# A gated cross-attention block with a quantised feed-forward part: fused mask and row maximum, deviations spread through DRAM, later transposes, another order of the last batches and of the barrier

## The chip, the cores and the metric

The kernel runs on one core of a Trainium2 chip. The metric is device time in microseconds (us), the median of repeated executions. PE is TensorE, DVE is VectorE, ACT is ScalarE, POOL is GpSimd, and SP is the engine that issues most of the transfers.

## The reference

Eight batches (B = 8) of 256 rows (S) of width 256 (D); the context has the same shape; the hidden width I is 704.

```python
# attention: q from layernorm(x), k and v from the context
qh, kh, vh = q @ Wq.T, k @ Wk.T, v @ Wv.T
scores = where(tril, qh @ kh.T / sqrt(256), -inf)
probs = softmax(scores, axis=1)          # over the queries
x = x + tanh(g_xattn) * (probs @ vh)
# feed-forward: every tensor is quantised to 8 bits and scaled back
xq = fake_quant(layernorm(x))            # ONE scale: the maximum over the whole tensor
gate, up = xq @ q(w_gate).T, xq @ q(w_up).T
h = fake_quant(silu(gate) * up)          # again one scale for all of it
x = x + tanh(g_ffn) * (h @ q(w_down).T)
```

The two scales over a whole tensor are barriers: nothing of the hidden layer can be quantised before the last batch's attention is through.

## The kernel before

The host hands over x by rows and x and the context transposed (`xc`), 8 batches each, and all weights. All of it is loaded once, by one list of transfers on SP's queue (lines 286 to 303) and five on ScalarE's (636 to 640), with no wait between them.

The weights Wq and Wk are multiplied into one matrix first (`a_sb`, line 492). Per batch b, on TensorE (loop at line 502):

- `scores(b)`, line 423: context times scaled queries `uT` into PSUM bank SC, transposed so that the softmax runs along the free dimension. It has two column ranges, 256 for the first 128 keys and 128 for the others. Behind each a small bf16 product of the identity and `causal` (line 429) adds -1e30 where the mask is.
- `values(b+2)`, line 396, and `project_queries(b+1)`, line 403, into bank U. The query rows still lack their layernorm factor.
- `spread_deviation(b+2)`, line 412: the factor 1/deviation (`rstd1`, one number per partition) is spread along a row by a product with the identity. ScalarE copies it to `r_bc` (line 644), and VectorE multiplies bank U by it into `uT` (`scale_queries_whole`, line 820).
- `attend(b)`, line 432, which waits for the exponentials and the scaled values, and `transposes2(b-1)`, line 443, the transposes of the second layernorm's result.

VectorE's loop (line 898) does, in this order: residual, statistics and variance of batch b-1 (lines 836 to 854), the two row maxima (826), statistics of batch b+3 (798), a weight maximum (865, or 912 for the down weights), the reciprocal of the softmax sum (832), weight scales, the variance of batch b+3 with its epsilon (806), the scaling of the queries (820), and the largest value of an earlier normalised batch (860). ScalarE's loop (698): exponentials, scaled values, `r_bc`, a copy of the transposes, and quantising one slot of the weights. GpSimd (345): the power -1/2 for both layernorms and the normalising of batches 0 to 5 (`apply2`, 338).

PSUM has eight banks: U, three for values, SC, AT (attention), X2 (transposes) and RB (spread deviations, later turned weights). The gate and up weights are turned by TensorE at batches 6 and 7, the down weights at batch 7, into banks that are free by then.

The last two batches' normalised rows are made by VectorE (line 857, used at 914 and 974). Then come the transposes of batch 7 in two halves (544), the spread of the maximum (`spread_max`, 473) with matmuls on ones around it that keep TensorE running (`keep_warm`, 385), act_scale and act_inv (979), and the quantising of the input (992 to 1019, ScalarE's share 744 to 751). The hidden layer, the second barrier and the down projection follow.

Of the kernel before, what the change touches and what calls it, by code (L numbers as in the profile page):

```python
# [50 lines left out]
def gated_block(nc, x, xc_in, wq_in, wk_in, wvT_in, scalars_in, wgu_in, wd_in, out):  # L51
    assert S == 256 and D == 256 and REST == P // 2 and B == 8 and HALF == 2 * CH

    with ExitStack() as stack:
# [26 lines left out]
        causal = sb("causal", [P, P], BF16)  # L81
# [11 lines left out]
        var1 = sb("var1", [P, B, QT])  # L93
        var2 = sb("var2", [P, B, QT])
        rstd1 = sb("rstd1", [P, B, QT])
        rstd2 = sb("rstd2", [P, B, QT])
        r_bc = [sb(f"r_bc{p}", [P, S]) for p in range(2)]
# [3 lines left out]
        inv_sum = sb("inv_sum", [P, B, QT])  # L101
        probs0 = [sb(f"probs0_{p}", [P, S]) for p in range(2)]
# [3 lines left out]
        xn2T = sb("xn2T", [P, KT, B * S])  # L106
        xmax = sb("xmax", [P, B + 1])
# [14 lines left out]
        wd_diag = sb("wd_diag", [P, KT, P])  # L122
# [21 lines left out]
        U, V0, V1, V2, SC, AT, X2, RB = range(8)  # L144
# [14 lines left out]
        def query_bank(b, f):  # L159

            return bank(V2)[:, 0:S] if b == 0 and f == 1 else bank2(U)[:, f, :]

# [37 lines left out]
        var1_done = sem("var1_done")  # L200
        rstd1_done = sem("rstd1_done")
# [17 lines left out]
        xn2_last = sem("xn2_last")  # L219
# [15 lines left out]
        wguT_last = sem("wguT_last")  # L235
        wd_tr = sem("wd_tr")
        wdT_ready = sem("wdT_ready")
        wd_diag_done = sem("wd_diag_done")
# [36 lines left out]
        def _(sp):  # L275
# [9 lines left out]

            sp.dma_start(ctxT(0), xc_in[0, :, 0]).then_inc(c_here[0], 16)
# [28 lines left out]
        def _(pool):  # L315
# [8 lines left out]
            nc.gpsimd.affine_select(out=causal[:], in_=causal[:], compare_op=ALU.is_ge, fill=MASKED, base=0,  # L324
# [13 lines left out]
            def apply2(b):  # L338
                pool.wait_ge(rstd2_done, b + 1)
# [7 lines left out]
            for b in range(B):  # L347
                if 1 <= b:
                    inverse_deviation2(b - 1)
                if 1 <= b < LAST:  # L350
                    apply2(b - 1)
                if b + 3 < B:
                    inverse_deviation1(b + 3)
            for t in range(QT):
                pool.wait_ge(var2_done, B + t)
                nc.gpsimd.tensor_tensor(rstd2[:, LAST, t:t + 1], var2[:, LAST, t:t + 1], minus_half[:, 0:1],
                                        ALU.pow).then_inc(rstd2_done, 1)

            pool.wait_ge(act_scale_done, 1)
            nc.gpsimd.tensor_scalar(gu_scale[:], wscale[:], act_scale[:, 0:1], None, ALU.mult).then_inc(  # L360
                gu_scale_done, 1)
# [9 lines left out]
            for half in range(2):  # L371
                nc.gpsimd.tensor_scalar(out_scale[:, half, :], wd_row[:], act_scale[:, 1:2], None,
                                        ALU.mult).then_inc(out_scale_done, 1)
# [10 lines left out]
        def _(pe):  # L384
# [27 lines left out]
            def spread_deviation(b):  # L412
# [4 lines left out]
                for t in range(QT):  # L417
                    last = nc.tensor.matmul(bank(RB)[:, t * P:(t + 1) * P],  # L418
# [4 lines left out]
            def scores(b):  # L423
                pe.wait_ge(uT_ready, KT * (b + 1))
                for k, (c0, n) in enumerate(((0, S), (S, P))):
                    for f in range(KT):
                        nc.tensor.matmul(bank(SC)[:, c0:c0 + n], ctxT(b)[:, f, k * P:(k + 1) * P],  # L427
                                         uT[b % 2][:, f, k * P:S], start=(f == 0), stop=False)
                    last = nc.tensor.matmul(bank(SC)[:, c0:c0 + P], ident_bf[:], causal[:], start=False, stop=True)
# [13 lines left out]
            def transposes2(b):  # L443
# [3 lines left out]
                for e in range(KT):  # L447
                    for t in range(QT):
                        last = nc.tensor.transpose(bank2(X2)[:, e, t * P:(t + 1) * P],  # L449
# [14 lines left out]
            def turn_down(n, bk):  # L464
                pe.wait_ge(wd_q_done, 1)
                view = ps[:, bk, :].bitcast(BF16)[:, 0:3 * D].rearrange("p (s h) -> p s h", s=3)
                for s in range(3):
                    i0 = (3 * n + s) * P
                    for t in range(KT):
                        last = nc.tensor.transpose(view[:, s, t * P:(t + 1) * P], wd_q[:, t, i0:i0 + P], ident_bf[:])  # L470
# [31 lines left out]
            for b in range(LAST):  # L502
                scores(b)
                if b + 2 < B:
                    values(b + 2)
                project_queries(b + 1)
                if b + 2 == LAST:
                    pe.wait_ge(wd_diag_done, 1)
                    pe.wait_ge(rbc_ready, LAST)
                    nc.tensor.matmul(bank(RB)[:, S:S + D], ones[:], wd_diag[:].rearrange("p t i -> p (t i)"),  # L510
                                     start=True, stop=True)
                if b + 2 < B:
                    spread_deviation(b + 2)
                if b + 1 == LAST:

                    turn_gate_up(0, VB[(b + 2) % 3])
                    pe.wait_ge(rbc_ready, B)
                    pe.wait_ge(wd_row_ready, 1)
                    turn_gate_up(1, RB)
                attend(b)  # L520
                if b >= 1:
                    transposes2(b - 1)

            p = LAST % 2
            last_value_bank = VB[LAST % 3]
            spare = VB[(LAST - 1) % 3]
            scores(LAST)
            turn_gate_up(2, U)
            turn_down(0, spare)
            pe.wait_ge(wguT_ready, 2)  # L530
            turn_down(1, RB)
            transposes2(LAST - 1)
# [11 lines left out]
            for t, bk in enumerate((last_value_bank, X2)):  # L544
                pe.wait_ge(xn2_last, t + 1)
                if bk == X2:
                    pe.wait_ge(xn2T_ready, LAST)
                for e in range(KT):
                    last = nc.tensor.transpose(bank(bk)[:, e * P:(e + 1) * P], xn2[p][:, t, e * P:(e + 1) * P],
                                               ident[:])  # L550
                last.then_inc(tr2_done, 1)
            spread_max(0, AT)
            keep_warm(WARM_AT_BARRIER, SC)


            pe.wait_ge(act_scale_done, 1)
            pe.wait_ge(wguT_ready, 2)
            pe.wait_ge(wguT_last, 1)
            pe.wait_ge(wdT_ready, 1)
            pe.wait_ge(xn2T_ready, B)  # L560
# [27 lines left out]
            for i in range(FULL):  # L588
                for half in range(2):
                    if i == 0 and half == 1:  # L590
                        pe.wait_ge(wdT_ready, 4)
# [544 lines left out]
```

## Time and profile before

| what | us |
|---|---|
| median of 3 runs (122.58 to 123.74) | 122.9 |
| profiled execution, its own time | 123.01 |
| span of its profile | 121.2 |
| busy in the span: PE | 109.7 |
| busy: DVE | 90.2 |
| busy: ACT | 69.7 |
| busy: POOL | 51.0 |

The span is what the profiler saw of the engines; the execution's own time also holds what lies around it. The busy times are sums over stages with different limits. The mean granted clock of TensorE was 0.994 of full.

### The profile page before, as it was taken

What the parts mean: (1) busy time and instruction counts of PE and PEld (TensorE: products, weight loads), DVE (VectorE), ACT (ScalarE), POOL (GpSimd) and SP (SyncE); (2) the same over time, 40 slices, a digit from 0 to 9 for tenths busy, and PEclk for the clock granted to TensorE, in tenths of its full rate; (3) what the DMA queues carried; (4) which work ended last, traced back from release to release, by engine and by line L of the source; (5) the groups of instructions that cost most, each with busy time, mean ns of one, the idle gap of its engine ahead of it and who ended that gap; (6) DMA issues with size and microseconds to landing.
All of it is one profiled execution on the core that took longest, in us unless ns stands there. A gap on an engine that the chain in (4) does not pass through costs nothing.

```text
span 121.2 us, 1874 instructions
## 1 busy us (share of the span) xinstructions
PE 109.7 (90%) x658; PEld 86.6 (71%) x660; DVE 90.2 (74%) x215; ACT 69.7 (58%) x127; POOL 51.0 (42%) x55
## 2 busy tenths in 40 slices
PE   6997999999999999999999797899999797878970
PEld 6885888888878888988878695644444386656750
DVE  0057377798979987667658697985999997888892
ACT  0401234354637488484686694988888820998700
POOL 6002222092752908446090212107666640677820
PEclk9999999999999999999999999999999999999997
DMA  3999999960000000000000000000000000023455
GB/s 91 354 329 417 422 416 406 412 269 8 0 0 0 3 5 0 0 0 0 0 0 5 0 0 0 0 3 5 0 0 0 0 0 0 0 77 122 156 173 173
DMA packets 5513, 11.65 MB, mean 96 GB/s; under 512 B 640, under 2 KB 2688, under 8 KB 5504
## 3 DMA queue, kind: packets, MB, share of 16 engines
q1 hardware_dynamic: 4784, 10.49, 23.0%
q10 hardware_dynamic: 720, 1.05, 2.5%
q8 instruction: 5, 0.08, 0.2%
q14 instruction: 4, 0.03, 0.1%
HBM read 9.44 MB, written 2.10 MB: 95 GB/s over the span
## 4 chain that ended last, share of the span: by engine, by line
PE 52%; DVE 25%; POOL 7%; DMA 6%; issue 5%; ACT 2%; ACTq 1%; DVEq 0%; POOLq 0%
PE ps L408 11%; PE ps L392 9%; PE ps L427 8%; DVE hmax L1030 8%; DMA xs<-in_x 6%; PE ps L626 4%; POOL hq L379 3%; DVE shared L1025 3%; PE ps L438 3%; PE ps L418 3%; PE ps L440 3%; PE ps L439 2%; PE ps L449 2%; PE ps L584 2%; POOL shared L366 2%
## 5 line engine op out<-in xcount | busy, mean ns | idle before, releaser
L584 PE MATMUL ps<-xq,wguT 128*128 128x512 bf16 x78 | 17.2, 379 | 0.5 <-DVE xq L999 0.4
L392 PE MATMUL ps<-wvT,shared 128*128 128x256 f32 x64 | 16.8, 408 | 0.0
L366 POOL TENSOR_TENSOR shared<-up_sb,silu 128x1024 f32<-128x1024 f32 x5 | 11.8, 2361 | 10.5 <-ACT up_sb L765 10.5
L341 POOL TENSOR_SCALAR xn<-xs,mv,rstd 128x256 f32<-128x256 f32 x12 | 14.9, 1251 | 0.6
L408 PE MATMUL ps<-shared,a_sb 128*128 128x256 f32 x64 | 15.2, 380 | 0.0
L336 POOL TENSOR_TENSOR rstd<-var,minus_half 128x2 f32<-128x2 f32 x7 | 4.9, 695 | 23.2 <-DVE var L854 23.2
L584 PEld LDWEIGHTS ps<-xq,wguT 128*128 128x128 bf16 x80 | 7.8, 98 | 9.6 <-issue 0.7
L388 PE MATMUL ps<-ones 128*128 128x128 f32 x98 | 13.7, 301 | 1.0 <-POOL ones L316 1.0
L388 PEld LDWEIGHTS ps<-ones 128*128 128x128 f32 x98 | 13.0, 214 | 1.5 <-POOL ones L316 1.0
L392 PEld LDWEIGHTS ps<-wvT,shared 128*128 128x128 f32 x64 | 12.5, 205 | 1.8
L408 PEld LDWEIGHTS ps<-shared,a_sb 128*128 128x128 f32 x64 | 12.0, 190 | 1.6
L1030 DVE TENSOR_REDUCE hmax<-shared 128x1 f32<-128x2048 f32 (+1 forms) x6 | 12.7, 2108 | 0.6 <-POOL shared L366 0.2
L427 PE MATMUL ps<-uT,shared 128*128 128x256 f32 (+1 forms) x64 | 12.8, 336 | 0.1
L626 PE MATMUL ps<-wdT,hq 128*128 128x256 bf16 x80 | 11.0, 274 | 1.9 <-POOL hq L379 1.3
L760 ACT ACTIVATE silu<-ps,gu_scale 128x1024 f32<-128x1024 f32 x10 | 11.1, 1115 | 1.8 <-PE ps L584 1.8
L332 POOL TENSOR_TENSOR rstd<-var,minus_half 128x2 f32<-128x2 f32 x8 | 5.6, 706 | 15.5 <-DVE var L812 15.3
L427 PEld LDWEIGHTS ps<-uT,shared 128*128 128x128 f32 x64 | 9.7, 191 | 1.7 <-DVE uT L817 0.3
L626 PEld LDWEIGHTS ps<-wdT,hq 128*128 128x128 bf16 x80 | 7.2, 98 | 4.7 <-POOL hq L379 3.0
L659 ACT ACTIVATE vh<-ps,inv_sum 128x256 f32<-128x256 f32 x16 | 6.7, 471 | 5.7 <-DVE inv_sum L834 5.7
L379 POOL TENSOR_SCALAR hq<-ints 128x1408 bf16<-128x1408 int16 x6 | 8.2, 1359 | 2.9 <-PE ps L627 2.7
L794 ACT ACTIVATE ints<-shared,act_inv 128x1408 int16<-128x1408 f32 x6 | 8.7, 1469 | 0.9 <-POOL hq L379 0.5
L839 DVE SCALAR_TENSOR_TENSOR xs<-ps,tanh_g,xs 128x512 f32<-128x512 f32 x7 | 5.3, 751 | 4.2 <-PE ps L440 4.2
(126 smaller groups left out, 199.0 us busy)
## 6 DMA issues: line engine op xcount, KB each, us to landing
shared<-in_xc SPq DMA_DIRECT2D x6, 512.0 KB, 14.7
out<-xs SPq DMA_DIRECT2D x7, 256.0 KB, 2.1
xs<-in_x SPq DMA_DIRECT2D x3, 512.0 KB, 11.9
shared<-in_wgu SPq DMA_DIRECT2D x3, 512.0 KB, 10.3
shared<-in_xc SPq DMA_DIRECT2D x3, 256.0 KB, 5.7
wd<-in_wd SPq DMA_DIRECT2D x1, 768.0 KB, 13.3
wvT<-in_wvT ACTq DMA_DIRECT2D x1, 256.0 KB, 3.7
wq_sb<-in_wq ACTq DMA_DIRECT2D x1, 256.0 KB, 4.8
```

Of the source, the lines that this page charges most:

```text
L341: last = nc.gpsimd.tensor_scalar(xn2[b % 2][:, t, :], xs[:, QT * b + t, :], mv2[:, b, t, 0:1], rstd2[:, b, t:t + 1], ALU.subtract, ALU.mult)
L366: nc.gpsimd.tensor_tensor(hid[:, 2 * i + 1, :], up_sb[i % 2][:], silu1[i % 2][:], ALU.mult).then_inc(hid_done[1], 1)
L379: nc.gpsimd.tensor_scalar(hq[c % 2][:], hq_i16[c % 2][:], QMAX, -QMAX - 1, ALU.min, ALU.max).then_inc(hq_clipped, 1)
L388: nc.tensor.matmul(bank(bk)[:, 0:P], ones[:], ones[:], start=True, stop=True)
L392: last = nc.tensor.matmul(bank2(VB[b % 3])[:, k, :], ctxT(b)[:, e, k * P:(k + 1) * P], wvT[:, e, :], start=(e == 0), stop=(e == KT - 1))
L408: last = nc.tensor.matmul(query_bank(b, f), a_sb[:, e, f * P:(f + 1) * P], xT(b)[:, e, :], start=(e == 0), stop=(e == KT - 1))
L427: nc.tensor.matmul(bank(SC)[:, c0:c0 + n], ctxT(b)[:, f, k * P:(k + 1) * P], uT[b % 2][:, f, k * P:S], start=(f == 0), stop=False)
L584: last = nc.tensor.matmul(bank(4 * half + 2 * g + c), wguT[:, i, g, k, :], xq[:, k, col:col + CH], start=(k == 0), stop=(k == KT - 1))
L626: nc.tensor.matmul(dst, hq[c % 2][:, 2 * i + half, :], wdT[:, i, :], start=(i == 0), stop=False)
L760: nc.scalar.activation(dst[:], ps[:, 4 * half:4 * half + 2, :].rearrange("p c n -> p (c n)"), ACT.Silu, scale=gu_scale[:, i, 0:1]).then_in ...
L794: nc.scalar.activation(hq_i16[c % 2][:], hid[:, :, c * P:(c + 1) * P], ACT.Copy, scale=act_inv[:, 1:2]).then_inc(hq_int_act, 1)
L1030: nc.vector.tensor_reduce(hmax[:, n:n + 1], hid[:, first:first + count, :].rearrange("p s n -> p (s n)"), AX.X, ALU.max, apply_absolute_va ...
```

## The change

1. **Mask and row maximum.** The two mask products per batch go. `causal` becomes a float tile of 256 columns, the last 128 zero. Row maxima are two `tensor_tensor_reduce`: they write -(score + mask) to SBUF (`neg_scores`) and its minimum along the row to `neg_max`. The exponentials read `neg_scores` with scale -1. TensorE's scores wait for the earlier batch's maximum.
2. **Deviations through DRAM.** For batches 2 to 7 SP waits for `rstd1`, stores it to DRAM (1 KB), and loads it back as a broadcast row of 256 to all partitions; `r_bc` has a row for every batch. The same is done once with the scale of the down weights. The loads of xc(3) and later stand behind these waits in SP's list. The product with `wd_diag` goes.
3. **Small work.** The epsilon of the first layernorm is added on GpSimd. The two statistics of the residual stand around the row maximum. The weight maxima and scales stand behind the reciprocal or behind the scaling of the queries, and slots 2 to 3 come in batch 0, slots 4 to 5 in batch 1. GpSimd's operations with one operation or a subtract become two operations of add and multiply; `apply2` needs a negated mean first, and normalises batch 6 as well.
4. **Transposes later.** `transposes2` lags by two batches. The gate and up weights are turned in batches 2, 4 and 5, the down weights in batches 6 and 7.
5. **Last batches and barrier.** scores(7) stands ahead of attend(6). For batch 7 ScalarE writes mean - x (`neg_dev`), VectorE takes its largest absolute value and multiplies it by the deviation factor; GpSimd makes the normalised rows. The transposes of batches 6 and 7 stand behind `spread_max`, their copies among the quantising.
6. On ScalarE's queue x of batch 0 goes ahead of its transposed x.

```diff
@@ SP
             load_wgu(1)
+            spread_deviation_out(2)
             load_xc(3)
+            spread_deviation_back(2)
             load_x(3)
+            load_wgu(2)
+            spread_deviation_out(3)
+            load_xc(4)
+            spread_deviation_back(3)
             sp.dma_start(wd[:], wd_in).then_inc(wd_here, 16)
-            load_xc(4)
-            load_wgu(2)
+            spread_deviation_out(4)
             load_xc(5)
+            spread_deviation_back(4)
             load_x(4)
+            spread_deviation_out(5)
             load_xc(6)
+            spread_deviation_back(5)
+            spread_deviation_out(6)
             load_xc(7)
+            spread_deviation_back(6)
+            spread_deviation_out(7)
+            spread_deviation_back(7)
+            sp.wait_ge(wdscale_done, 1)
+            sp.dma_start(down_spread, wdscale[:]).then_inc(wd_spread_out, 16)
+            sp.wait_ge(wd_spread_out, 16)
+            sp.dma_start(wd_spread[:], everywhere(down_spread)).then_inc(wd_spread_here, 16)
@@ GpSimd
             def inverse_deviation1(b):
+                pool.wait_ge(mv1_done, b + 1)
+                nc.gpsimd.tensor_scalar(var1[:, b], mv1[:, b, :, 1], LN_EPS, 1.0, ALU.add, ALU.mult).then_inc(
+                    var1_done, 1)
...
             def apply2(b):
+                nc.gpsimd.tensor_scalar(neg_mean[:, b], mv2[:, b, :, 0], -1.0, 1.0, ALU.mult, ALU.mult).then_inc(
+                    neg_mean_done, 1)
...
-                    last = nc.gpsimd.tensor_scalar(xn2[b % 2][:, t, :], xs[:, QT * b + t, :], mv2[:, b, t, 0:1],
-                                                   rstd2[:, b, t:t + 1], ALU.subtract, ALU.mult)
+                    last = nc.gpsimd.tensor_scalar(xn2[b % 2][:, t, :], xs[:, QT * b + t, :], neg_mean[:, b, t:t + 1],
+                                                   rstd2[:, b, t:t + 1], ALU.add, ALU.mult)
...
+            pool.wait_ge(var2_done, B)
+            nc.gpsimd.tensor_tensor(rstd2[:, LAST], var2[:, LAST], minus_half[:], ALU.pow).then_inc(rstd2_done, 1)
+            pool.wait_ge(rstd2_done, B)
+            pool.wait_ge(neg_dev_done, QT)
             for t in range(QT):
+                last = nc.gpsimd.tensor_scalar(xn2[LAST % 2][:, t, :], neg_dev[:, t, :], rstd2[:, LAST, t:t + 1], -1.0,
+                                               ALU.mult, ALU.mult)
+            last.then_inc(xn2_ready, 1)
@@ TensorE
-            for b in range(LAST):
+            for b in range(LAST - 1):
                 scores(b)
-                if b + 2 < B:
-                    values(b + 2)
+                values(b + 2)
                 project_queries(b + 1)
+                if b == 2:
+                    pe.wait_ge(rbc_ready, 2)
+                    turn_gate_up(0, WT)
+                if b == 4:
+                    pe.wait_ge(wguT_ready, 1)
+                    turn_gate_up(1, WT)
+                if b == 5:
+                    pe.wait_ge(wguT_ready, 2)
+                    turn_gate_up(2, WT)
+                if b >= 2:
+                    transposes2(b - 2)
                 attend(b)
+            scores(LAST - 1)
+            project_queries(LAST)
+            pe.wait_ge(wguT_ready, 3)
+            turn_down(0, WT, range(0, 4))
+            transposes2(LAST - 3)
             scores(LAST)
+            attend(LAST - 1)
+            transposes2(LAST - 2)
+            turn_down(1, spare, range(4, SLOTS))
...
             keep_warm(WARM_BEFORE_MAX, AT)
             spread_max(0, AT)
+            transposes2(LAST - 1)
+            pe.wait_ge(wdT_ready, 1)
+            pe.wait_ge(xn2_ready, B)
+            for e in range(KT):
+                for t in range(QT):
+                    last = nc.tensor.transpose(bank2(WT)[:, e, t * P:(t + 1) * P],
+                                               xn2[p][:, t, e * P:(e + 1) * P], ident[:])
+            last.then_inc(tr2_done, 1)
             keep_warm(WARM_AT_BARRIER, SC)
@@ VectorE
             def row_max(b):
                 dve.wait_ge(scores_done, b + 1)
-                nc.vector.tensor_reduce(neg_max[:, b, 0:1], bank(SC)[:, 0:S], AX.X, ALU.max, negate=True)
-                nc.vector.tensor_reduce(neg_max[:, b, 1:2], bank(SC)[:, S:S + P], AX.X, ALU.max,
-                                        negate=True).then_inc(max_done, 1)
+                for k, (c0, n) in enumerate(((0, S), (S, P))):
+                    last = nc.vector.tensor_tensor_reduce(neg_scores[b % 2][:, c0:c0 + n], bank(SC)[:, c0:c0 + n],
+                                                          causal[:, 0:n], -1.0, -MASKED, ALU.add, ALU.min,
+                                                          accum_out=neg_max[:, b, k:k + 1])
+                last.then_inc(max_done, 1)
...
+            for b in range(LAST):
                 if b >= 1:
                     residual(b - 1)
+                    stats2(b - 1, 0)
+                row_max(b)
+                if b >= 1:
+                    stats2(b - 1, 1)
                     variance2(b - 1)
                 if b + 3 < B:
                     stats1(b + 3)
...
                 invert_sum(b)
                 if b + 3 < B:
                     variance1(b + 3)
+                if b == 0:
+                    weight_max(0)
+                if b == 1:
+                    weight_max(2)
...
+                scale_queries_whole(b + 1)
+                if b == 0:
+                    weight_scale(0)
+                    weight_max(1)
+                    weight_scale(1)
+                if b == 1:
+                    weight_scale(2)
+                if b == 2:
...
+                if b >= 2:
+                    largest2(b - 2)
+            row_max(LAST)
+            largest2(LAST - 2)
+            residual(LAST - 1)
+            stats2(LAST - 1, 0)
+            invert_sum(LAST)
+            stats2(LAST - 1, 1)
+            variance2(LAST - 1)
...
+            largest2(LAST - 1)
             for t in range(QT):
+                dve.wait_ge(neg_dev_done, t + 1)
+                nc.vector.tensor_reduce(dev_max[:, t:t + 1], neg_dev[:, t, :], AX.X, ALU.max,
+                                        apply_absolute_value=True).then_inc(dev_max_done, 1)
+            dve.wait_ge(dev_max_done, QT)
+            dve.wait_ge(rstd2_done, B)
+            nc.vector.tensor_tensor(xmax[:, LAST:LAST + QT], dev_max[:], rstd2[:, LAST], ALU.mult).then_inc(xmax_done, 1)
...
             input_clip(1, 1)
+            dve.wait_ge(tr2_done, LAST)
+            nc.vector.tensor_copy(xn2T[:, :, (LAST - 1) * S:LAST * S], bank2(X2)).then_inc(xn2T_ready, 1)
@@ ScalarE
+            act.wait_ge(tr2_done, B)
+            nc.scalar.copy(xn2T[:, :, LAST * S:B * S], bank2(WT)).then_inc(xn2T_ready, 1)
+            act.wait_ge(xn2T_ready, B)
             nc.scalar.activation(xq_i16[:, :, 3 * CH:4 * CH], xn2T[:, :, 3 * CH:4 * CH], ACT.Copy,
                                  scale=act_inv[:, 0:1]).then_inc(xq_int_act, 1)
```

## Rows read from the trace of the kernel before

**Rows 1.** The page, part 4: the chain's shares by engine.
```profile
PE 52%; DVE 25%; POOL 7%; DMA 6%; issue 5%; ACT 2%; ACTq 1%; DVEq 0%; POOLq 0%
```

**Rows 2.** The chain in order of time, attention: start us, length us, what.
```profile
14.87 1.13 PE ps L427 x4
...
30.25 0.06 PE ps L429
30.30 0.50 PE ps L427 x4
...
30.86 1.78 PE ps L392 x8
32.64 1.73 PE ps L408 x8
34.37 0.45 PE ps L418 x4
34.81 0.14 issue
34.95 0.67 PE ps L438 x2
...
36.05 0.43 PE ps L440 x2
36.49 0.44 PE ps L449 x4
...
56.24 0.43 PE ps L510 x2
...
58.85 0.86 PE ps L427 x4
...
62.11 0.89 PE ps L460 x16
```

**Rows 3.** VectorE in order of time, one batch: start, busy us, instruction, [idle before].
```profile
21.98 0.75 DVE L839 SCALAR_TENSOR_TENSOR xs<-ps,tanh_g,xs 128x512 f32<-128x512 f32 x1 [1.07 <-PE ps L440]
...
23.91 0.42 DVE L828 TENSOR_REDUCE neg_max<-ps 128x1 f32<-128x256 f32 x1
24.45 0.74 DVE L803 BATCH_NORM_STATS2 bn<-xs 128x6 f32<-128x256 f32 x2
25.11 1.20 DVE L867 TENSOR_REDUCE wmax<-shared 128x4 f32<-128x1024 f32 x1
...
27.17 0.69 DVE L823 TENSOR_TENSOR uT<-ps,r_bc 128x512 f32<-128x512 f32 x1
27.78 0.68 DVE L862 TENSOR_REDUCE xmax<-xn 128x1 f32<-128x512 f32 x1
```

**Rows 4.** The page, part 6: transfers, KB each, median us from issue to landing.
```profile
shared<-in_xc ACTq DMA_DIRECT2D x1, 256.0 KB, 6.6
...
out<-xs SPq DMA_DIRECT2D x2, 128.0 KB, 1.7
```

**Rows 5.** All engines in order of time, start-up.
```profile
10.19 1.03 PE L392 MATMUL ps<-wvT,shared 128*128 128x256 f32 x4
```

**Rows 6.** ScalarE in order of time, the same batch.
```profile
25.28 0.20 ACT L651 ACTIVATION_READ_ACCUMULATOR probs<-ps,neg_max 128x1 f32 x1
26.47 0.84 ACT L659 ACTIVATE vh<-ps,inv_sum 128x256 f32<-128x256 f32 x2 [0.99 <-DVE inv_sum L834]
```

**Rows 7.** The chain in order of time, barrier.
```profile
74.70 0.17 DVE col_max L982
...
75.83 0.17 DVE act_inv L987
...
77.47 2.55 PE ps L584 x11
```

**Rows 8.** Groups of instructions: busy us, mean ns of one, idle before.
```profile
L341 POOL TENSOR_SCALAR xn<-xs,mv,rstd 128x256 f32<-128x256 f32 x12 | 14.9, 1251 | 0.6
...
L379 POOL TENSOR_SCALAR hq<-ints 128x1408 bf16<-128x1408 int16 x6 | 8.2, 1359 | 2.9 <-PE ps L627 2.7
```

More of the change, by code:

```diff
@@ L96, in gated_block @@
         rstd2 = sb("rstd2", [P, B, QT])
-        r_bc = [sb(f"r_bc{p}", [P, S]) for p in range(2)]
+        r_bc = sb("r_bc", [P, B, S])
         uT = [sb(f"uT{p}", [P, KT, S]) for p in range(2)]
@@ L101, in gated_block @@
         inv_sum = sb("inv_sum", [P, B, QT])
+        neg_scores = [sb(f"neg_scores{p}", [P, S + P]) for p in range(2)]
         probs0 = [sb(f"probs0_{p}", [P, S]) for p in range(2)]
@@ L200, in gated_block @@
         var1_done = sem("var1_done")
+        spread_out = sem("spread_out")
+        r_here = [sem(f"r_here{b}") for b in range(2, B)]
+        wd_spread_out = sem("wd_spread_out")
+        wd_spread_here = sem("wd_spread_here")
+        neg_mean_done = sem("neg_mean_done")
+        neg_dev_done = sem("neg_dev_done")
+        dev_max_done = sem("dev_max_done")
         rstd1_done = sem("rstd1_done")
@@ L696, in _, with wdT_out, wdT_rest_out @@
             deviation_out(1)
+            def wdT_out(bk):
+                act.wait_ge(wd_tr, 1)
+                nc.scalar.copy(wdT[:, 0:4, :].rearrange("p s h -> p (s h)"),
+                               ps[:, bk, :].bitcast(BF16)).then_inc(wdT_ready, 1)
+            def wdT_rest_out(bk):
+                act.wait_ge(wd_tr, 2)
+                view = ps[:, bk, :].bitcast(BF16)
+                nc.scalar.copy(wdT[:, 4, :], view[:, 0:D]).then_inc(wdT_ready, 1)
+                act.wait_ge(rest_zeroed, 1)
+                for half in range(2):
+                    rows = slice(half * REST, (half + 1) * REST)
+                    nc.scalar.copy(wdT_rest[rows, half, :], view[rows, D:2 * D]).then_inc(wdT_ready, 1)
             for b in range(LAST):
@@ L732, in _ @@
-            act.wait_ge(wd_tr, 2)
-            nc.scalar.copy(wdT[:, 3:5, :].rearrange("p s h -> p (s h)"),
-                           ps[:, RB, :].bitcast(BF16)[:, 0:2 * D]).then_inc(wdT_ready, 1)
-            last_xn2T_out(0, VB[LAST % 3])
-            act.wait_ge(rest_zeroed, 1)
-            for half in range(2):
-                rows = slice(half * REST, (half + 1) * REST)
-                nc.scalar.copy(wdT_rest[rows, half, :],
-                               ps[rows, RB, :].bitcast(BF16)[:, 2 * D:3 * D]).then_inc(wdT_ready, 1)
@@ L741, in _ @@
-            last_xn2T_out(1, X2)
+            xn2T_out(LAST - 2)
+            wdT_rest_out(VB[(LAST - 2) % 3])
+            for t in range(QT):
+                act.wait_ge(mv2_done, LAST + t + 1)
+                nc.scalar.activation(neg_dev[:, t, :], xs[:, NT - QT + t, :], ACT.Identity, bias=mv2[:, LAST, t, 0:1],
+                                     scale=-1.0).then_inc(neg_dev_done, 1)
+            nc.scalar.activation(silu0[:, 0:1], scalars[:, 0:1], ACT.Silu).then_inc(silu_loaded, 1)
             act.wait_ge(act_inv_done, 1)
-            act.wait_ge(xn2T_ready, LAST)
+            act.wait_ge(xn2T_ready, LAST - 1)
@@ L896, in _ @@
             variance1(2)
-            for b in range(B):
+            dve.wait_ge(consts, 3)
+            for b in range(LAST):
                 if b >= 1:
```

253 lines of the change are left out of this document (99 added, 154 removed).

## Prediction

> **What bounds the kernel now.** I read the chain that ended last first: half of it is TensorE, a quarter VectorE [rows 1]. In order of time it splits the kernel into four stretches. Until 14.87 us it is a start-up sequence; from there to about 64 us it is almost unbroken TensorE work, one batch after another; from 64 to 77.5 us it hops between engines at the barrier (the global maximum); behind that comes the hidden layer, which the change leaves alone. For the attention stretch the reader is to see the pieces of one batch [rows 2]: scores (0.86 and 0.50 us, and two masks of 0.06), values 1.78, query projection 1.73, deviations spread by TensorE 0.45, attention three times 0.43, transposes 0.44. Scores of batch 6 start at 58.85. So six batches took 58.85 - 14.87 = 43.98 us. VectorE's order of time for one batch [rows 3] shows it nearly as full: from the residual at 21.98 to the end of the last maximum at 28.46 it hardly pauses, 6.5 us of a batch of 7.4. That is what the change has to be weighed against: work taken from TensorE helps only as far as VectorE follows.
>
> **The change, part by part.** The profiled execution (123.01 us, span 121.2) is the base; it lies 0.1 above the median 122.9.
>
> *Start.* The rows for batch 0 now go out ahead of its transposed x on ScalarE's queue. That transfer was issued 0.5 us earlier and took 6.6 us [rows 4], so the rows can be there near 8.3 instead of 9.75. VectorE is free by then. GpSimd now adds the epsilon too, an instruction that I put at 0.3 us against 0.17 on VectorE. The deviation would be there near 10.5, but TensorE is in its value matmuls until 10.19 + 1.03 = 11.22 [rows 5]. Its spreading moves from 11.94 to 11.22: **-0.7**. The transposed x, now second, should land near 9.8, before its use at 11.9. Bounds: 0 if the swap changes nothing, -0.9 at best.
>
> *TensorE's work, batches 0 to 5* [rows 2]. Masks out: 6 x 0.12 = 0.72. Six spreadings out: 6 x 0.44 = 2.64, and the down-weight spreading, 0.43. One batch of transposes fewer falls in this stretch, 0.44, since they now lag by two batches. Two short waits (0.12 and 0.14) and the slow first attend behind each (0.67 for 0.43) come to 0.74. Added: three gate/up turns, 3 x 0.89 = 2.67, which stood at 62.11 and behind. 43.98 - 0.72 - 2.64 - 0.43 - 0.44 - 0.74 + 2.67 = 41.7 us, if nobody makes TensorE wait.
>
> *VectorE, the price of the fused row maximum.* The two reduces occupy 0.54 (23.91 to 24.45) [rows 3]. No row shows the new instruction. A two-operand pass over 512 PSUM columns takes 0.69 there, which scales to about 0.42 for 256 columns, the same as the reduce. The written accumulator must cost something; ScalarE pays 0.20 for reading one, though 0.1 of it overlaps [rows 6]. I take 0.75 for the pair, with 0.54 and 1.8 (each pass at half rate, with a separate read-out) as ends.
>
> *VectorE, the schedule.* With r counted from the start of scores(0): row maximum 1.75 to 2.5, statistics (0.66) to 3.2, exp of some 0.95 behind the maximum (its end at 24.53, the last read's at 25.48) [rows 3, 6], reciprocal to 3.7, aggregates to 4.0, first weight maximum (1.1) [rows 3] to 5.1, scaling of the queries at u_done 5.2 to 5.9. Then the code puts the other weight work: scale 0.5, the second weight maximum 1.1, scale 0.5, ending at 7.9. TensorE is through batch 0 at 6.4. So the residual starts 1.4 late; it, the row maximum, statistics and aggregates (0.79 + 0.39 + 0.75 + 0.39 + 0.37 + 0.66) put the reciprocal of batch 1 at 11.4 and the scaled values (0.84 plus hand-over) [rows 6] at 12.35, where TensorE wanted them at 11.3: it waits **1.0 us**. Batch 2 follows at 13.65. The down-weight maximum (half again as wide as the 1.20 row, about 1.7) lies in batch 2, which is also longer on TensorE by one turn (0.89); VectorE enters batch 3 0.8 late, and batch 3 has just room for that (values scaled at 26.4, TensorE ready at 26.5). Batches 4 and 5 have a turn each as slack. Scores(6) start at r = 42.8 instead of 43.98: **-1.2**.
>
> *Epsilon moved to GpSimd, statistics split in two, order of weight work:* VectorE gains 0.1 a batch; included above.
>
> *The round trip through DRAM.* Each of six deviations waits on SP for GpSimd, goes out, comes back as a broadcast, and loads are queued behind these waits. The nearest rows are the 128 KB stores, 1.7 us [rows 4]. SP reaches the first such wait after its ninth load, and GpSimd has that deviation near 16.2. So xc(3) is issued at about 16.7 and lands near 20, where TensorE wants it at 22.0. The broadcast is back at 21 for a use at 26.9; x for batches 4 and 5, issued near 19, is wanted at 24.8. Later trips have 6 us or more. Cost 0; if one trip took over 4 us instead of 2, the x load would be the first late one, and TensorE would stand. The rule that speaks against this part is in the Trainium skill, "DMA: Bandwidth & Descriptors", section on latency: HBM access averages 0.2 us but 2 us at high load. The queue has been drained by 16 us here (its first nine loads and ScalarE's four are 4.3 MB), so no row of before shows a store under load; by the rule a trip would be a few us longer, which the third rival prices in its own way.
>
> *The tail, from scores(6), called T.* Before: T = 58.85, barrier done (end of act_inv) at 76.0 = T + 17.15, first gate matmul 77.47, both halves of slot 0 at 80.02 = T + 21.17 [rows 7]. After: scores(6) to 1.4, projection 3.1, down turn and transposes 4.0, VectorE scales batch 7 until 4.0, scores(7) 4.1 to 5.5, attend(6) to 6.8. VectorE: row maximum(7) to 6.3, a maximum to 7.0, residual(6) 7.8, reciprocal(7) 8.3, variance(6) 9.05. TensorE attends batch 7 from 8.8 (values scaled) to 10.2. Residual, statistics, aggregate of its two halves: 9.5 to 12.05. The maximum of batch 6 (0.68) and two of the deviations (0.35 and 0.42) go to 13.4, then the small product and the column maximum to 13.8. Column maximum's end to act_inv's end took 1.15 before; with its hand-over, T + 14.9. Normalising batch 7 and its transposes lie behind the maximum now. But they stand ahead of the keep-warm matmuls on TensorE: 0.47 spread, 0.88 transposes, 1.5 warming end at 16.8, later than the first quantised input (14.9 + 1.45). Gate starts at 16.8, slot 0 ends at 19.35: **-1.8**.
>
> *GpSimd's forms.* Each pass over 256 elements took 1.25 us with subtract and multiply; the min/max pass over 1408 took 1.36, 0.97 ns an element [rows 8]. The new form is two operations of add/multiply kind. Between 0.55 (0.3 fixed plus 256 x 0.97) and 1.25 I take 0.55: like the quick row it has two operations and no subtract. At 1.25, the last normalisation ends at T + 15.8 instead of 13.9, and the gate starts at 17.9: +1.1.
>
> Sum: 123.01 - 0.7 - 1.2 - 1.8 = 119.3, and 119.2 against a median of 122.9.
>
> The Trainium skill, "VectorE: DVE Perf Modes", in the section on two Vector instructions with no wait between them, says that an op which also writes out its accumulator is two instructions. The ScalarE row agrees in kind (a separate read of 0.20), none shows it for VectorE. Without the rule the pair would cost 0.54, with it 0.75 or more; both are inside the bounds taken.
>
> **Rivals.**
> (a) *VectorE becomes the bound; slower.* If the fused pair costs c instead of 0.54, it is paid on the chain twice in batches 0 and 1, once in batch 3 and twice in the tail, five times in all; my sum holds 5 x 0.21 already. Gain gone at c = 0.75 + 3.7/5 = 1.5. At c = 1.75: 119.3 + 5 x 1.0 = 124.3 us. For: no row shows the instruction, and VectorE is nearly full [rows 3]. Against: a two-operand PSUM pass is as quick as a reduce.
> (b) *GpSimd's new forms are no quicker.* 120.3 us, by the +1.1 above. For: the nearest row by operands is the 1.25 one.
> (c) *The round trip is late.* Trips of 5 to 6 us hold up x for batches 4 and 5 and the loads behind: about 3 us, 122.2, no change worth the name. Against: more than 5 us of room for each broadcast.
> (d) *TensorE stays the bound:* VectorE's 1.0 stall in batch 1 does not come and the pair costs 0.6: 119.2 - 1.0 - 0.7 = 117.5.
>
> **Chances.** Forecast (118.3 to 120) 0.45, (b) 0.17, (d) 0.15, (c) 0.13, (a) 0.10. A measurement here tells about 1% (1.2 us) from no change. The forecast, (b) and (d) are faster by more: 0.77. Most of (c) is within 1%, 0.13 with the mild cases of (a). Slower by over 1%: 0.10. The range takes (d) as its low end and most of (c) as its high end: 117.3 to 122.3.
>
> **What would show it.** Scores(0) starting near 14.2. A row-maximum pair of 0.7 to 0.8 on VectorE. A TensorE wait near 1 us ahead of attend(1) and none over 0.3 in batches 3 to 5. Batch 4 taking about 7.5 us with its turn and batch 3 about 6.6. Broadcasts landing at least 4 us before their use. act_inv about 15 us after scores(6). From the first quantised input the rest of the kernel as long as before. It is wrong if the pair costs over 1.2 us, if TensorE waits for a load or a broadcast, if GpSimd's pass stays at 1.25, or if batches 3 to 5 are bound by VectorE.

## The result, and the profile after

The changed kernel takes 129.5 us (median of 4 runs, 127.8 to 130.7) against 122.9 before, a ratio of 1.044 (95% interval 1.037 to 1.051). It is slower, and lies 7 us above the top of the range. The ratios, here and below, leave out the executions more than 1.5% above the fastest of their kernel, and the medians count them all. The profiled execution took 127.81, span 126.0.

The page of the changed kernel, parts 1, 2 and 4 (busy time; tenths by slice of 3.15 us; shares of the chain):

```profile
PE 108.0 (86%) x616; PEld 84.4 (67%) x618; DVE 87.3 (69%) x217; ACT 68.6 (54%) x121; POOL 46.6 (37%) x74
...
PE   6999998739999429999999549999999797879980
...
PEclk9999999999999995999999986999999999999999
DMA  3999685994874928310601000000000000004554
...
DMA 30%; DVE 21%; PE 21%; POOL 10%; issue 7%; ACT 6%; SPq 2%; DVEq 0%; POOLq 0%; ACTq 0%
```

Before, transfers were 6% of the chain and TensorE 52% [rows 1]; now transfers are 30% and TensorE 21%. TensorE's row has holes at the digits 7 3 (from 22 us), 4 2 (from 41) and 5 4 (from 69), and behind the last two its granted clock drops (5, then 8 6): it was 0.50 from 48 to 50 us and again from 75 to 78. The loads, with the trips between them, go on past 47 us, where the last one leaves (in experiment 1 below the last one lands at 28.6).

The chain in order of time, changed kernel (start, length, what) says which transfers:

```profile
15.97 3.42 DMA spread<-rstd
...
20.73 8.46 DMA spread<-rstd
...
29.58 7.40 DMA wd<-in_wd
...
42.44 4.09 issue
...
55.96 2.82 DMA spread<-rstd
...
59.16 5.59 DMA down_spread<-wdscale
...
64.77 4.27 DMA wd_spread<-down_spread
```

A kilobyte stored to DRAM takes 2.8 to 8.5 us here until it has landed. The page, part 6, and the view of transfers (median us from issue to landing):

```profile
shared<-in_xc SPq DMA_DIRECT2D x6, 512.0 KB, 6.8
...
xs<-in_x SPq DMA_DIRECT2D x3, 512.0 KB, 6.7
...
r_bc<-spread SPq DMA_DIRECT2D x6, 128.0 KB, 5.1
wd<-in_wd SPq DMA_DIRECT2D x1, 768.0 KB, 7.4
...
spread<-rstd SPq DMA_DIRECT2D x6, 1.0 KB, 5.8
```

I had reckoned a store and its broadcast at 2 us each; they take 5.8 and 5.1. SP stands still for the store, and each load behind it in the list leaves that much later. SP's DMA queue in order of time, changed kernel:

```profile
22.18 1.33 SPq L297 DMA_DIRECT2D shared<-in_xc  x1
29.21 0.33 SPq L309 DMA_DIRECT2D r_bc<-spread  x1
29.58 2.41 SPq L328 DMA_DIRECT2D wd<-in_wd  x1
32.03 0.43 SPq L305 DMA_DIRECT2D spread<-rstd  x1
...
37.55 0.33 SPq L309 DMA_DIRECT2D r_bc<-spread  x1
37.92 0.43 SPq L294 DMA_DIRECT2D xs<-in_x  x1
```

Ahead of these lines, xc(3) left at 16.34 and x for batches 4 and 5 at 19.78, as I had them, but took 6.3 and 6.7 us. (With SP's waits and no store, experiment 16, xc(3) takes 3.3.) The x load at 37.92 is that for batches 6 and 7. VectorE, which works in order, stands for each x with a reciprocal queued behind that TensorE needs. VectorE and then TensorE in order of time (start, busy, instruction, [idle before <- what ended it]):

```profile
26.52 0.75 DVE L852 BATCH_NORM_STATS2 bn<-xs 128x6 f32<-128x256 f32 x2 [2.40 <-DMA xs<-in_x]
...
44.68 0.75 DVE L852 BATCH_NORM_STATS2 bn<-xs 128x6 f32<-128x256 f32 x2 [2.45 <-DMA xs<-in_x]
45.35 0.15 DVE L889 RECIPROCAL inv_sum<-row_sum 128x2 f32<-128x2 f32 x1
```

```profile
22.72 1.99 PE L447 MATMUL ps<-wvT,shared 128*128 128x256 f32 x8 [1.08 <-DMA shared<-in_xc]
...
28.38 0.67 PE L494 MATMUL ps<-vh,probs 128*128 128x256 f32 x2 [1.94 <-issue]
...
29.75 1.53 PE L484 MATMUL ps<-uT,shared 128*128 128x256 f32 x8
...
46.53 0.67 PE L494 MATMUL ps<-vh,probs 128*128 128x256 f32 x2 [4.11 <-issue]
...
48.42 2.63 PE L484 MATMUL ps<-uT,shared 128*128 128x256 f32 x8
```

The three waits are 7.1 us. The trace puts the longest down to "issue", that is to no releaser, but attend needs ScalarE's scaled values, which start at 45.59, behind the reciprocal of 45.35, and end at 46.4. After the longest wait, the same eight score matmuls take 2.63 instead of 1.53: the granted clock is 0.50 there. Scores(6) start at 63.48, 49.5 us behind scores(0) at 14.01, where I had 42.8 (and before it was 43.98).

The barrier pays once more. GpSimd waits 7.1 us for the broadcast of the down-weight scale, with the normalising of the last batches queued behind. The chain from 69.04 (that broadcast's landing) on:

```profile
70.56 1.09 POOL xn L388 x2
...
71.67 0.69 DVE xmax L914
72.36 0.67 DVE xs L894
...
73.64 0.48 ACT vh L710
74.12 0.09 issue
74.22 0.75 PE ps L589 x2
```

The normalised rows' maximum stands ahead of the reciprocal for batch 7 on VectorE, so the last attention starts at 74.22. Slot 0 ends at 85.48 = T + 22.0, predicted T + 19.35, before T + 21.17. From there to the end of the span it is 40.5 us, 41.2 before.

### The profile page after: what moved, and what is told of

The parts are those of the page before. It is cut to its first block, busy times and chain, and to the rows that moved or that the text cites. A ratio compares the mean times of both kernels' runs of the same rounds, so it can differ in the third digit from the quotient of the medians.

```text
span 126.0 us, 1829 instructions
## 1 busy us (share of the span) xinstructions
PE 108.0 (86%) x616; PEld 84.4 (67%) x618; DVE 87.3 (69%) x217; ACT 68.6 (54%) x121; POOL 46.6 (37%) x74
## 4 chain that ended last, share of the span: by engine, by line
DMA 30%; DVE 21%; PE 21%; POOL 10%; issue 7%; ACT 6%; SPq 2%; DVEq 0%; POOLq 0%; ACTq 0%
DMA spread<-rstd 12%; DVE hmax L1087 7%; DMA wd<-in_wd 6%; DMA shared<-in_xc 5%; DMA down_spread<-wdscale 4%; PE ps L443 4%; DMA wd_spread<-down_spread 3%; POOL hq L434 3%; DVE shared L1082 3%; PE ps L676 3%; PE ps L634 2%; PE ps L484 2%; POOL shared L421 2%; POOL xn L388 2%; PE ps L447 2%
## 5 line engine op out<-in xcount | busy, mean ns | idle before, releaser
L380 POOL TENSOR_TENSOR rstd<-var,minus_half 128x2 f32<-128x2 f32 x7 | 5.1, 725 | 28.2 <-DVE var L910 28.2
L443 PE MATMUL ps<-ones 128*128 128x128 f32 x98 | 14.5, 312 | 1.0 <-POOL ones L357 1.0
L443 PEld LDWEIGHTS ps<-ones 128*128 128x128 f32 x98 | 14.0, 227 | 1.6 <-POOL ones L357 1.0
L484 PEld LDWEIGHTS ps<-uT,shared 128*128 128x128 f32 x64 | 11.7, 208 | 2.2 <-DVE uT L874 0.4
L700 ACT ACTIVATE probs<-neg_scores,neg_max 128x256 f32<-128x256 f32 x8 | 4.0, 506 | 12.3 <-DVE neg_max L882 12.3
L852 DVE BATCH_NORM_STATS2 bn<-xs 128x6 f32<-128x256 f32 x16 | 6.0, 416 | 5.8 <-DMA xs<-in_x 5.6
L494 PE MATMUL ps<-vh,probs 128*128 128x256 f32 x14 | 4.3, 391 | 6.0 <-issue 6.0
```

The costliest lines, as they stand in the source:

```text
L443: nc.tensor.matmul(bank(bk)[:, 0:P], ones[:], ones[:], start=True, stop=True)
L484: last = nc.tensor.matmul(bank(SC)[:, c0:c0 + n], ctxT(b)[:, f, k * P:(k + 1) * P], uT[b % 2][:, f, k * P:S], start=(f == 0), stop=(f == K ...
```

## Experiments

T is again the start of scores(6). "Before" was run beside each kernel, at 122.9 to 123.3. The experiments stood on five chips, so times of different chips are best compared by their ratios to before. Two theories stood at the start: the trips through DRAM cost the time, or VectorE does, with its fused pair and new order.

**1. Spreading by TensorE again, no trips.** The rest of the change stays.

```diff
 load_wgu(1)
-spread_deviation_out(2)
 load_xc(3)
-spread_deviation_back(2)
 load_x(3)
 load_wgu(2)
-spread_deviation_out(3)
...
 project_queries(b + 1)
+spread_deviation(b + 2)
```

> The changed kernel with the six deviations spread by TensorE again, and the loads issued with no wait between them; all else as changed, the down-weight trip too. Theory O (the waits and trips in SP's list hold loads back, and VectorE and TensorE wait for them): about 121 us; TensorE has 6 x 0.44 more work, and no wait for a load is left. Rival R (the rest of the change makes VectorE the bound): 126 us or more, with TensorE's long waits still ahead of attend in batches 1 and 3.

Measured: 119.6 us (119.5 to 119.9), ratio 0.973 (0.971 to 0.976). The page, clock and DMA rows:

```profile
PEclk9999999999999999999999999999999999999999
DMA  3989999991000320000000000000000000023555
```

All loads are in by 28.6 us and the mean granted clock is 1.000. TensorE is busy for 49.8 of the 50 us from 14 to 64. Scores(0) start at 14.54, T is 57.73 with 2.6 us of spreading in it, and slot 0 ends at 77.20 = T + 19.5. The span is 117.7, 8.3 less than the changed kernel's: 5.75 by T, 2.5 in the tail. VectorE, with all its new work, isn't to blame.

**2. SP's waits alone.** As 1, but SP still waits for each deviation where the change does, without storing or fetching anything.

```diff
-spread_deviation_out(b)
+sp.wait_ge(rstd1_done, b + 1)
-spread_deviation_back(b)
```

> As e1, but SP keeps its waits for each deviation ahead of the loads; no store and no broadcast is issued. Theory O1 (the transfers of the trip are what costs, by their landing time and by what they hold up): the deviations come early enough, so within 1 us of e1, about 121. Rival O2 (already the waits for the deviations make loads late): half the loss or more stays, 125 us or more.

Measured: 119.5 (119.4 to 119.9), ratio 0.972 (0.969 to 0.975). Holding back the loads until GpSimd has each deviation costs nothing. It is the transfers of the trips.

**3. Broadcasts that read 128 different rows.** Trips and waits stay; each broadcast, the one of the down-weight scale too, reads 128 rows of a weight, so the values used are others.

```diff
-sp.dma_start(r_bc[:, b], everywhere(spread[b]))
+sp.dma_start(r_bc[:, b], wk_in[:, 0, :])
```

> The changed kernel, but each broadcast reads 128 different rows of 1 KB of a weight instead of one row 128 times (the factors are then wrong numbers; sizes, waits and order stay). Theory S (128 reads of the same 1 KB are slow and hold up the loads beside them): the landing falls from 5.1 us to under 3, the loads behind arrive earlier, 126 us or less. Rival (it is the small store, or the latency of any transfer): landing and time as changed, 129.5.

Measured: 120.6 (119.4 to 123.1), 0.977 (0.969 to 0.985). Broadcasts land in 3.7 us, not in under 3 as I expected of this theory; the time falls by more than it asked for.

**4. One weight row read 128 times.** As 3 with `wk_in[0:1, 0, :]` broadcast to all partitions, again other values. It asks if it is the many reads of one row, or that the row was just written.

> As e3, but each broadcast reads one and the same 1 KB row of a weight 128 times; nothing has just written it. Theory H (many reads of one row are what is slow): landing near 5 us and 127 to 129.5 us, as the changed kernel. Rival F (reading what a store has just written is slow): landing 3.7 us or less and about 120.6 us, as e3.

Measured: 120.4 (119.5 to 121.8), 0.982 (0.975 to 0.989), as quick as 3, though the broadcasts land in 4.3 us, between 3's 3.7 and the changed kernel's 5.1. That one row is read 128 times is not what costs the time.

**5. Decoys.** Experiment 1 with six such one-row broadcasts among the loads, unused.

> e1 (no trips, 119.6 us) with six broadcasts of one weight row put among the loads where the trips' broadcasts stood, with no wait on or behind them. Theory H: while each is under way the loads move little, so every load behind it lands 3 to 4 us later than in e1; the second weight loads and x have room for one of them, and the time is 119.6 to 122. Rival (reads of one row do not hold up the others): landings as in e1, 119.6.

Measured: 119.8 (119.2 to 119.9), 0.972 (0.968 to 0.976). Such reads don't slow the loads about them: the xc loads land in 14.0 us (14.9 in experiment 1), the x loads in 12.3 (12.8).

**6. GpSimd's wait for the down-weight row moved** behind the first work of the hidden layer; everything else as changed.

```diff
-if b == 5:
-    pool.wait_ge(wd_spread_here, 16)
...
+pool.wait_ge(wd_spread_here, 16)
...
 pool.wait_ge(wd_row_ready, 1)
```

> The changed kernel with GpSimd's wait for the down-weight row, 7.1 us long, moved from batch 5 to just ahead of the row's use behind the hidden layer. Theory: the wait holds the normalised rows of batch 5, for which VectorE (1.9 us) and TensorE (1.3 us) wait ahead of the barrier, so 127.3 us, 2 to 2.5 less. Rival: the last batches' chain hides it, 129.5 us.

Measured: 126.7 (126.5 to 128.2), 1.033 (1.027 to 1.040), 2.8 us less than the changed kernel by the medians, 1.3 by the ratios. The trace shows the tail's part: slot 0 ends at T + 19.5 instead of T + 22.0, so 2.5 us. But T itself came 1.3 us later in this execution (64.81 for 63.48), so 2.5 is read from the trace, and the times alone don't show it.

**7. The fused maximum undone** inside experiment 1: masks on TensorE, plain reduces, exponentials from PSUM.

> e1 with masks on TensorE and the two plain reduces again. Theory (the fused pair costs VectorE nothing, as the profile after shows: 0.55 us against 0.54): undoing it adds only the two masks, 0.12 us a batch, 120.5 us. Rival (the fused form costs more than it saves, by the exponentials' read from SBUF): 119.6 or less.

Measured: 121.2 (120.9 to 121.5), 0.984 (0.981 to 0.988). The fused pair is worth 1.6 us here by the medians, 1.4 by the ratios, more than the masks' 1.0 (8 x 0.12).

**8. All loads first, trips last.** Batch 2's deviation by TensorE, those of 3 to 7 through DRAM behind every load; GpSimd's wait as in 6.

```diff
-spread_deviation_out(2)
 load_xc(3)
-spread_deviation_back(2)
 load_x(3)
...
 load_xc(7)
+spread_deviation_out(3)
+spread_deviation_back(3)
...
+spread_deviation_out(7)
+spread_deviation_back(7)
```

> The changed kernel with all loads issued ahead of every trip, the deviation of batch 2 spread by TensorE (its trip would come too late behind the loads), those of batches 3 to 7 through DRAM, and the wait for the down-weight row moved behind the hidden layer. Theory (a trip is harmless where no load stands behind it and its result has time): 119.6 of e1 less 5 x 0.44 for TensorE, 117.4 us. Rival (the trips' slow transfers still cost, by their own lateness): 119.6 or more.

Measured: 117.9 (117.6 to 118.2), ratio 0.958 (0.954 to 0.961), faster than both kernels. Its trips still take 4.9 and 4.1 us (store and broadcast), but SP's queue shows why nobody waits:

```profile
19.75 0.33 SPq L305 DMA_DIRECT2D spread<-rstd  x1
29.00 0.33 SPq L309 DMA_DIRECT2D r_bc<-spread  x1
...
42.38 0.32 SPq L305 DMA_DIRECT2D spread<-rstd  x1
46.04 0.32 SPq L309 DMA_DIRECT2D r_bc<-spread  x1
```

The first store, issued into a full queue, takes over 9 us; with no load behind it, that is free.

**9. Experiment 8 with the order on ScalarE's queue as before** (transposed x first).

> e4 (117.9 us) with x of batch 0 again behind its transposed x on ScalarE's queue. Theory (the swap moves the spread of the first deviation ahead by 0.7 us): 118.6. Rival (the transfer of context 1, for which TensorE waits until 8.5 in e4, now sets the start, so that the swap brings little): 117.9 to 118.2.

Measured: 118.0 (117.6 to 118.2), 0.959 (0.956 to 0.962). The swap brings nothing there.

**10. An old row.** All of the trips stay, but every broadcast reads `spread[0]`, stored once ahead of the first trip, so all batches are scaled by the first one's deviation. That row's own store and SP's wait for it come on top.

> The changed kernel with its stores, waits and order, but every broadcast reads one row of the scratch tensor that was stored once, ahead of the first trip, and not touched again (factors of batch 0 for all batches). Theory F (what has just been stored is slow to read): the broadcasts land in 3.7 to 4.3 us as in e3 and e7, about 120.5 us. Rival P (the scratch tensor itself is slow to read, wherever it lies): landings near 5 us, 127 to 129.5 us.

Measured: 120.7 (119.8 to 122.5), 0.979 (0.974 to 0.984); broadcasts 3.1 us, stores 5.0.

**11. Each broadcast one trip later,** so that its row is older, with the right row.

> The changed kernel, all six trips kept, but each broadcast is issued one trip later in SP's list, behind the next store and its loads, so that the row it reads was stored 5 us or more before and no load of x waits for a store's landing (each store has a semaphore of its own for that). Theory F (a row just stored is slow to read, an older one is not): broadcasts land in about 3 us when no load stands ahead of them, and the time is 118 to 120.5 us. Rival (every row stored by these small stores is slow to read): landings near 5 us, 124 us or more.

Measured: 121.4 (120.5 to 124.9), 0.981 (0.975 to 0.987), above most of what I expected. The profiled execution lay 3.5 us over the median, so nothing is read from its trace, and this run doesn't settle what age does.

**12. The changed kernel beside it.**

> The changed kernel itself once more, on the same chip as e12, to see how far its landings and its time spread: 127.8 to 130.7 us as before, the broadcasts' landing again near 5 us. If it came out near 121, the comparison with e3, e7 and e10 would have to be thrown out.

Measured: 125.3 (123.6 to 127.3), a ratio of medians of 1.016. On this chip it is 4 us quicker than in the first runs; the kernel before is not (123.3). Counted as the other ratios are, by its two quickest executions (123.6 and 124.3), it comes to 1.005, hardly any loss, and experiment 11 gained 2.9 on it rather than the 3.9 of the medians. In the execution profiled here (123.64) TensorE's longest wait is 2.67 us, its mean granted clock is 1.00, and the span is 121.9.

**13 to 16. A ladder on one chip:** the changed kernel, 10, stores and their landing waits alone (factors by TensorE, no broadcast of a deviation), and 2.

> The changed kernel, as the base for e15 and e16 on the same chip: between the 125.3 and the 129.5 us of its two earlier measurements. Both theories take it as given; the differences of e15 and e16 to it are what is read.

> e10 once more, beside the changed kernel on one chip. Theory F (the broadcasts' reads of a row just stored are a large part of the loss): at least 3 us under e14, 120 to 121.5, its broadcasts landing 1 us or more earlier. Rival (the difference lay between the chips): within 1 us of e14.

> The six stores and SP's waits for their landing where the changed kernel has them, but no broadcasts; the factors come by TensorE (6 x 0.44 us more work for it), so it compares with e2 (waits for the deviations only, 119.5) and, for the rest, with e15. Theory F: stores and their landing waits cost 1 to 2 us over e2, 120.5 to 121.5, and the rest of the loss is the broadcasts'. Rival W (already waiting for the stores to land is what makes the loads late): 124 us or more.

> e2 once more, beside the others on the same chip: 119.5 us, the base for what the stores cost in e16.

| kernel | us | ratio (95%) | store, broadcast, xc, x, down weights: us to landing | DMA share, 14 to 64 us |
|---|---|---|---|---|
| waits only | 119.6 | 0.971 (0.966 to 0.976) | none, none, 3.5, 5.2, 7.8 | 0.30 |
| + stores | 121.1 | 0.982 (0.976 to 0.989) | 5.4, none, 6.6, 5.4, 5.5 | 0.47 |
| + broadcasts, old row | 122.2 | 0.992 (0.988 to 0.996) | 5.1, 3.4, 6.5, 5.7, 6.2 | 0.51 |
| + broadcasts, row just stored (changed) | 128.1 | 1.040 (1.033 to 1.047) | 5.7, 4.8, 7.4, 6.6, 7.4 | 0.59 |

The landings and shares are of one execution each, of 119.6, 119.9, 121.0 and 128.6 us. With the stores alone the xc load behind each takes nearly twice as long, and the 16 DMA engines are busy for 0.47 of the stretch instead of 0.30, at 108 and 107 GB/s. So the small stores keep the engines busy without moving more bytes.

The window from 14 to 64 us of the changed kernel on that chip, of the old-row kernel and of the one with stores only (PE, PEld, DVE, ACT, POOL busy; clock; DMA share; GB/s):

```profile
14.00:64.00 50.00, 42.31 (x215) 36.36 (x216) 32.53 (x112) 24.99 (x62) 15.51 (x32) 0.93 0.59 121
```

```profile
14.00:64.00 50.00, 46.61 (x263) 40.46 (x262) 37.41 (x126) 29.57 (x72) 16.55 (x34) 1.00 0.51 124
```

```profile
14.00:64.00 50.00, 49.18 (x284) 43.42 (x284) 37.30 (x127) 32.42 (x78) 18.03 (x37) 1.00 0.47 108
```

The waits for x and for the values (us in total, times, longest), first the changed kernel, then the old row's:

```profile
DVE bn L852 <- DMA xs<-in_x: 5.9, 3, 2.8
PE ps L494 <- issue: 5.3, 2, 4.2
```

```profile
DVE bn L856 <- DMA xs<-in_x: 3.2, 3, 1.5
```

The stores cost 1.5 us; the broadcasts of an old row add 1.1, although they free TensorE of six spreadings (2.6). That they read a row just stored adds 5.9: broadcasts 1.4 us slower in the median, stores and loads 0.6 to 1.2 us slower, and all of it one behind the other in SP's list. Not every broadcast is slower: the last of the six took 4.2 us in the changed kernel and 5.2 with the old row. In the two profiled executions TensorE is busy 4.3 us longer of the same 50 with the old row, and its clock stays at 1.00 there.

A good part of the 5.9 is the clock's. The mean granted clock is 0.973 over 126.8 us in the changed kernel and 0.994 over 119.2 with the old row, which is 3.4 and 0.7 us of full clock lost (my estimate from these numbers; it costs time only where TensorE is what the rest waits for). The execution of experiment 12, at a clock of 1.00, spans 121.9. The old-row kernel has slower executions too, 122.5 to 122.6 us at a clock of 0.97 to 0.99.

## Why the prediction was wrong

**The step that failed** is "the round trip through DRAM ... Cost 0". I sized a trip by the 128 KB stores to the output, 1.7 us [rows 4], which leave at the end, with no load beside them. A trip measured 5.8 + 5.1 us. "The queue has been drained by 16 us here" held for the first trip alone, and even that one took 3.4 us for its store and 5.5 for its broadcast; from then on each trip has the loads released ahead of it beside it, past 47 us. Load isn't all of it: behind all loads, in experiment 8, store and broadcast still take 4.9 and 4.1. The Trainium skill, "DMA: Bandwidth & Descriptors", section on latency, names 2 us for a memory access at high load. By that figure I had estimated a trip a few us longer; the trace agrees in direction, with trips of 11 us. The second fault is in "later trips have 6 us or more": the room was counted for each trip by itself. SP's list is one chain of waits, so lateness adds up: the second trip's store alone (20.73 to 29.19) holds its broadcast, the down weights and all that follows, and x for batches 6 and 7 leaves at 37.9. I wrote that beyond 4 us a trip the x load would be late first and TensorE would stand; xc(3) was late before it, by 1.1, because the 1 KB store ahead of it made a load of 3.3 us one of 6.3, and the rest went so.

**Rival (c)** had this mechanism, but with "trips of 5 to 6 us" where they took 11, and priced it at 3 us. My 0.10 for "slower" was VectorE's alone, rival (a). On the ladder the trips cost 8.5 (128.1 - 119.6), net of the 2.6 of spreading that they save. The rival left out that a transfer late on VectorE is paid by TensorE through the reciprocal; that TensorE's clock fell behind a 4 us pause; and the down-weight row on GpSimd, 2.5 us by the trace of experiment 6.

**What held.** The tail: T + 19.5 in experiment 1, predicted T + 19.35. GpSimd's pass: 558 ns, predicted 0.55, before 1251 [rows 8]; rival (b) fell. (The prediction took 0.55 from a pass of another kind, min and max, so that the size is right to 1% is partly luck.) Rival (a) fell too: experiment 7 shows a gain from the pair, and in experiment 1 TensorE is busy 49.8 of 50 us. The rows of the pair, groups of the changed kernel, and VectorE in order of time:

```profile
L388 POOL TENSOR_SCALAR xn<-xs,neg_mean,rstd 128x256 f32<-128x256 f32 x14 | 7.7, 558 | 0.7
...
L882 DVE DVE_READ_ACCUMULATOR2_ANT neg_max<- 128x1 f32 x16 | 1.3, 83 | 0.0
```

```profile
15.73 0.42 DVE L882 CUSTOM_DVE_ANT_0 neg_scores<-ps,causal 128x256 f32<-128x256 f32 x1 [0.84 <-PE ps L484]
16.08 0.08 DVE L882 DVE_READ_ACCUMULATOR2_ANT neg_max<- 128x1 f32 x1
16.08 0.28 DVE L882 CUSTOM_DVE_ANT_0 neg_scores<-ps,causal 128x128 f32<-128x128 f32 x1
16.29 0.08 DVE L882 DVE_READ_ACCUMULATOR2_ANT neg_max<- 128x1 f32 x1
16.29 0.75 DVE L852 BATCH_NORM_STATS2 bn<-xs 128x6 f32<-128x256 f32 x2
```

A fused pass of 256 columns takes 0.42, as the plain reduce did [rows 3]. The read-out is an instruction of its own, as the Trainium skill, "VectorE: DVE Perf Modes", section on two Vector instructions with no wait between them, says of an op that writes out its accumulator; the trace agrees (L882, 83 ns). But it lies beside the next pass: the pair takes 0.56 (15.73 to 16.29) against 0.54.

**Sizes that were off,** all to the pessimistic side. The pair: 0.75 for 0.56. A gate/up turn: 0.89 for 0.45 (34.57 to 35.02 on TensorE of the changed kernel). The row of 62.11 is x16 [rows 2], two calls of eight matmuls, so my three turns are 1.3 too much. The stall in batch 1: 1.0 for about 0.1 in experiment 1; part of it came from the price of the pair. Hence experiment 8, the change with its trips out of the way, comes out at 117.9, near rival (d)'s 117.5 and under my 119.2.

**The start:** scores(0) at 14.01 for 14.2, so 0.86 earlier than before. But it hangs on the transfer of the context of batch 1, which took 5.9 us there, 6.5 in experiments 1 and 12 and 6.9 in 8, with scores(0) at 14.54, 14.57 and 14.94. Experiment 12 is the changed kernel itself, so that 14.2 was met by luck in part, and the swap brings nothing in experiment 9.

**Open:** why a row just stored is slow to fetch, and slows what lies beside it. Many readers of one row are excluded (4, 5). The ladder shows that which row is read decides, but not how. The quick broadcasts (3, 4, 10, 14) read the same row, or the same 128, each time, the slow ones a new one each time; so "never read before" is a rival to "just stored" that nothing here tells apart. A fresh row fetched with a varied delay and nothing else in the queue was not tried. Open too is why the changed kernel took 125.3 on one chip and 128.1 to 129.5 on others, while the kernel before moved by 0.4. The traces show what goes with it: the longest pause of TensorE is 2.67 us at a clock of 1.00 in the one, 4.1 to 4.2 us and a mean clock of 0.97 in the others.

## What to carry to other kernels

Don't put a round trip through DRAM ahead of loads in an in-order list of DMAs: issue all loads first, then the trips (experiment 8: 117.9 for 129.5, much the same work). A wait for a computed result ahead of the loads cost nothing here (experiment 2), as the results were early enough. Size a small trip by a small transfer in a loaded queue, and add up lateness along the list. When a matmul row counts x16, look how many calls that is before multiplying.

## Of the hardware, not expected

- A store of 1 KB (128 partitions, 8 bytes each) takes 2.8 to 8.5 us to land. With such a store just ahead of it, a 512 KB load takes 6.6 us instead of 3.5 (experiments 15 and 16). Broadcasts of a row just stored take 4.8 us in the median, those of one old row 3.4, on one chip.
- GpSimd's `tensor_scalar` over 256 columns with add and multiply takes 558 ns, with subtract and multiply 1251 [rows 8]. The scalar operand changed too, from a column of `mv2` to `neg_mean`, and the two were not tried apart.
- Behind a pause of 4.11 us TensorE's granted clock fell to 0.50 for some 3 us; behind pauses of 1.1, 1.9 and (experiment 12) 2.67 us it didn't. The length of one pause doesn't tell: in the changed kernel it fell to 0.50 also behind pauses of 1.28 and 1.64 us with 0.9 us of work between them, and in its execution on the ladder's chip it didn't behind 1.08 and 1.64.
